# Edge phase of a graph-attention kernel: one f32 product for each query step and each relation step, with f32 one-hots

## What is computed

```python
mod_k  = K[src] + 0.2 * rel_w[edge_type][:, None, :]
scores = einsum('ehd,ehd->eh', Q[dst], mod_k) / 8
ex     = exp(scores - segment_max(scores, dst)[dst])
w      = ex / segment_sum(ex, dst)[dst]
agg    = segment_sum(w[:, :, None] * V[src], dst)
```

## Time and profile before

| | |
|---|---|
| median of three runs | 1356.09 us (1348.56 to 1357.88) |
| the profiled execution | 1346.19 us, span 1344.4 us |
| TensorE busy, share of the span | 1080.3 us, 80% |
| VectorE | 894.0 us, 66% |
| ScalarE | 666.2 us, 50% |
| GpSimd | 716.4 us, 53% |
| TensorE clock granted, mean | 0.868 of full speed |
| moved by DMA | 215.77 MB, mean 160 GB/s |

### The profile page before, as it was taken

How to read it: one execution, slowest core, us unless ns; L and a number is a source line. 1 busy time by engine, 2 the same in 40 slices (tenths; PEclk the granted TensorE clock), 3 DMA queues, 4 the chain that set the end, 5 groups by cost and what they waited for, 6 DMA issues and landing times.

```text
span 1344.4 us, 23897 instructions
## 1 busy us (share of the span) xinstructions
PE 1080.3 (80%) x7032; PEld 851.6 (63%) x7033; DVE 894.0 (66%) x1856; ACT 666.2 (50%) x2365; POOL 716.4 (53%) x714
## 2 busy tenths in 40 slices
PE   8978567776767777676677777799599999999997
PEld 3445345555545555555555565567389999999996
DVE  4767767677777877777777768889944444444443
ACT  5532356667667776576676766557511111111111
POOL 4455555555555655555556554756055555445663
PEclk9997777778888978777878878897699999999999
DMA  6266666656766666567666665602744444655332
GB/s 211 94 180 189 195 196 192 202 183 178 221 189 206 193 194 204 179 202 210 198 199 198 174 208 142 202 5 92 256 119 118 100 100 95 184 150 130 53 52 28
DMA packets 112993, 215.77 MB, mean 160 GB/s; under 512 B 19403, under 2 KB 57211, under 8 KB 112891
## 3 DMA queue, kind: packets, MB, share of 16 engines
q0 software_dynamic: 47488, 132.68, 36.7%
q1 hardware_dynamic: 59973, 80.16, 18.4%
q10 hardware_dynamic: 5430, 1.73, 0.6%
HBM read 191.96 MB, written 22.54 MB: 160 GB/s over the span
## 4 chain that ended last, share of the span: by engine, by line
PE 49%; DVE 21%; issue 16%; another core or an unknown queue 9%; ACT 2%; DMA 1%; DVEq 1%; SPq 0%; POOL 0%; POOLq 0%
PE qe_ps L1920 13%; PE bank L1929 8%; PE qe_ps L1732 6%; DVE ring L881 6%; PE bank L1772 5%; PE bank L1920 4%; DVE acc L893 3%; PE qe_ps L1772 2%; DVE ring L875 2%; DVE score L887 2%; PE qe_ps L1837 1%; PE qe_ps L1650 1%; PE qe_ps L1909 1%; PE bank L1650 1%
## 5 line engine op out<-in xcount | busy, mean ns | idle before, releaser
L632 POOL DMA_INDIRECT ring<-kv_table,src_idx x440 | 421.0, 957 | 330.4 <-DVE ring L881 181.5
L1502 ACT ACTIVATE wv<-ring,wgt 128x64 f32<-128x64 f32 x1628 | 407.3, 338 | 52.9 <-remote 46.5
L1732 PE MATMUL qe_ps<-q,hot_t 128*128 x1320 | 237.1, 316 | 140.0 <-issue 87.6
L1732 PEld LDWEIGHTS qe_ps<-q,hot_t 128*128 128x128 bf16 x1320 | 134.6, 110 | 209.0 <-issue 179.3
L1772 PE MATMUL bank<-wv,hotf 128*128 128x260 f32 x588 | 188.6, 451 | 25.2 <-issue 18.8
L697 POOL DMA_INDIRECT out<-room,slot_i x64 | 119.2, 1863 | 154.9 <-DMA out<-room,slot_i 81.4
L1920 PEld LDWEIGHTS qe_ps<-xg_t,ring 128*128 128x128 f32 x1536 | 181.4, 192 | 4.9 <-issue 1.7
L1621 ACT ACTIVATE act<-qe_ps 128x512 f32<-128x512 f32 x64 | 38.2, 597 | 294.7 <-PE bank L1920 140.9
L875 DVE TENSOR_TENSOR ring<-ring,bank 128x1024 f32<-128x1024 f32 x110 | 133.3, 1212 | 75.8 <-remote 63.3
L1920 PE MATMUL qe_ps<-xg_t,ring 128*128 128x128 f32 x1536 | 182.0, 275 | 1.3 <-issue 0.7
L881 DVE TENSOR_TENSOR ring<-ring,qe_ps 128x512 f32<-128x512 f32 x220 | 148.8, 677 | 26.1 <-remote 18.2
(11 more groups left out here) (339 smaller groups left out, 1504.5 us busy)
## 6 DMA issues: line engine op xcount, KB each, us to landing
ring<-in_w SPq DMA_DIRECT2D x48, 512.0 KB, 7.1
t_row<-t_rows SPq DMA_DIRECT2D x55, 256.0 KB
d_row<-d_rows SPq DMA_DIRECT2D x55, 256.0 KB
ring<-kv_table,src_idx POOLq DMA_INDIRECT x440
kv_table<-ring SPq DMA_DIRECT2D x25, 256.0 KB, 2.0
out<-acc SPq DMA_DIRECT2D x26, 128.0 KB, 1.7
x_table<-ring SPq DMA_DIRECT2D x26, 128.0 KB, 1.9
ring<-in_x SPq DMA_DIRECT2D x12, 256.0 KB, 9.0
```

Of the source, the lines that this page charges most:

```text
L632: pool.indirect_dma_start(ring[:, u, place(g) * D:(place(g) + 2) * D], None, kv_table, bass.IndirectOffsetOnAxis(ap=src_idx[:, 4 * g + u:4 ...
L1502: ins = act.activation(wv[:, g % WV_N, u, h, 0:HD], v_rows(g)[:, u, h * HD:(h + 1) * HD], ACT.Copy, scale=w[:, col:col + 1])
L1732: ins = pe.matmul(q_ps[p % AHEAD][:, u * D:(u + 1) * D], hot_t[:, p // 4 % HB_N, hot_cols(p, u)], tile_of(q3, q_tiles[p % 4])[:, k * D:(k ...
```

## The change

Queries are kept whole: `q_all`, f32, one copy from PSUM per tile by ScalarE (`keep_q`); the middle and low pieces, and VectorE's part in them, are gone. `hot_t` and `hot_r` become f32. `queries` makes one f32 product per step (two per pair), `relations` one f32 product per step with `rel_k`, `[64, 64]`; types, their one-hot and relation weights are on 64 partitions only. `turn_hot` still transposes bf16, reading the upper half of each f32 element. `hot_t` goes from seven buffers to six, and the copy of its first column for `factors` moves one octet ahead. Buffers move accordingly (`w_o`, `gamma`, `beta` and the gate's weights into `later`), and GpSimd no longer makes the relation's pieces. The core of the diff:

```diff
-HB_N = 7
+HB_N = 6
...
-        q3 = sb("q3", [P, NODE_TILES, 3 * D], BF16)
+        q_all = sb("q_all", [P, NODE_TILES, D])
+        later = sb("later", [P, KC * D + 2 * D + KC * NX + NX])
...
-        t_row = eb("t_row", [P, 8 * P], BF16)
-        hot_t = eb("hot_t", [P, HB_N, 8 * P], BF16)
-        hot_r = eb("hot_r", [P, 8 * P], BF16)
+        t_row = eb("t_row", [R, 8 * P], BF16)
+        hot_t = eb("hot_t", [P, HB_N, 8 * P])
+        hot_r = eb("hot_r", [R, 8 * P])
...
-                    c(pool.tensor_tensor(rel_r[:, :], rel02[:, :], rel_h[:, :], ALU.subtract))
-                    c(pool.tensor_copy(rel_m[:, :], rel_r[:, :]))
-                    c(pool.memset(rel_b[:, :], 0.0))
-                    c(pool.tensor_copy(rel_a[0:R, :], rel_h[0:R, :]))
-                    c(pool.tensor_copy(rel_a[R:P, :], rel_m[R:P, :]))
-                    c(pool.tensor_tensor(rel_b[0:R, :], rel_r[0:R, :], rel_m[0:R, :], ALU.subtract))
...
-                v.tensor_scalar(hot_r[:, :], t_row[:, :], part_r[:, 0:1], None, ALU.is_equal).then_inc(a_typ.sem, 1)
+                v.tensor_scalar(hot_r[:, :], t_row[:, :], part_r[0:R, 0:1], None, ALU.is_equal).then_inc(a_typ.sem, 1)
...
-            pieces_of_q(0, Q_FIRST)
...
                 if rows_due:
                     factor_rows(rows_due)
-                    v.tensor_copy(first[:, :], hot_t[:, rows_due * CS // 8 % HB_N, 0:1])
+                if maxima_due:
+                    v.tensor_copy(first[:, :], hot_t[:, maxima_due * CS // 8 % HB_N, 0:1])
...
-                sp.dma_start(t_row[:, :], bcast(t_rows[8 * m:8 * m + 8, :].rearrange("s c -> (s c)"))).then_inc(s_tr, 16)
+                sp.dma_start(t_row[:, :], bcast(t_rows[8 * m:8 * m + 8, :].rearrange("s c -> (s c)"), R)).then_inc(s_tr, 16)
...
-            def high_piece(t):
+            def keep_q(t):
                 s_q.wait(act, t)
-                act.activation(q3[:, t, 0:D], q_bank(t), ACT.Copy).then_inc(s_high.sem, 1)
...
+                act.activation(q_all[:, t, :], q_bank(t), ACT.Copy).then_inc(s_qk.sem, 1)
...
-                s_lo.wait(pe, min(p, NODE_TILES - 1))
+                s_qk.wait(pe, min(p, NODE_TILES - 1))
                 for u in range(2):
-                    for k in range(3):
-                        ins = pe.matmul(q_ps[p % AHEAD][:, u * D:(u + 1) * D], hot_t[:, p // 4 % HB_N, hot_cols(p, u)], tile_of(q3, q_tiles[p % 4])[:, k * D:(k + 1) * D],
-                                        start=(k == 0), stop=(k == 2))
+                    ins = pe.matmul(q_ps[p % AHEAD][:, u * D:(u + 1) * D], hot_t[:, p // 4 % HB_N, hot_cols(p, u)], tile_of(q_all, q_tiles[p % 4]), start=True, stop=True)
...
                 for u in range(8):
-                    for a in (rel_a, rel_b):
-                        ins = pe.matmul(rel_ps[:, u * HD:(u + 1) * HD], hot_r[:, u * P:(u + 1) * P], a[:, :], start=(a is rel_a), stop=(a is rel_b))
+                    ins = pe.matmul(rel_ps[:, u * HD:(u + 1) * HD], hot_r[:, u * P:(u + 1) * P], rel_k[:, :], start=True, stop=True)
...
-                    ins = pe.transpose(turn_ps.bitcast(BF16)[:, u * P:(u + 1) * P], hot_t[:, o % HB_N, u * P:(u + 1) * P], identb[:, :])
+                    ins = pe.transpose(turn_ps.bitcast(BF16)[:, u * P:(u + 1) * P], hot_t[:, o % HB_N, u * P:(u + 1) * P].bitcast(BF16)[:, 1::2], identb[:, :])
```

More of the change, by code:

```diff
@@ L294, in build @@
         rel = carve(acc_flat, HD)
-        rel02 = carve(acc_flat, HD)
-        rel_r = carve(acc_flat, HD)
         link_f = carve(acc_flat, CHUNKS * CS + 1)
         hop_f = carve(acc_flat, 2 * CHUNKS * CS).rearrange("p (i s) -> p i s", i=2)
-        rel_h = carve(acc_flat, HD // 2, BF16)
-        rel_m = carve(acc_flat, HD // 2, BF16)
         assert at[0] <= NT * H * HB
-        q3_flat = q3[:, :, :].rearrange("p t c -> p (t c)").bitcast(F32)
+        x_again = q_all[:, :, :].rearrange("p t c -> p (t c)")
+        xre = q_all[:, :, :]
         at[0] = 0
[L306 to L313, removed]
+        w_o = carve(later, KC * D).rearrange("p (k n) -> p k n", k=KC)
+        gamma = carve(later, D)
+        beta = carve(later, D)
+        gate_w = carve(later, KC * NX).rearrange("p (k n) -> p k n", k=KC)
+        gate_b = carve(later, NX)
         w_expert = flat[:, 0:WB * WX].rearrange("p (b n) -> p b n", b=WB)
@@ L357, in build @@
         typ = carve(hot_flat, STEPS // 2, BF16)
-        assert at[0] <= HB_N * 4 * P
+        first_row = carve(hot_flat, P)
+        last_row = carve(hot_flat, P)
+        iota_w = carve(hot_flat, P, I32)
+        iota_s = carve(hot_flat, 8, I32)
+        qe = carve(hot_flat, KC)
+        assert at[0] <= HB_N * 8 * P
         dst_t = late[0:PP, 0:4 * P].rearrange("p (q c) -> p q c", q=4)
@@ L457, in build @@
         s_xn, s_xt, s_enh, s_mm, s_ev, s_kv = (Count(sem(n)) for n in ("s_xn", "s_xt", "s_enh", "s_mm", "s_ev", "s_kv"))
-        s_q, s_high, s_rest, s_mid, s_lo = (Count(sem(n)) for n in ("s_q", "s_high", "s_rest", "s_mid", "s_lo"))
+        s_q, s_qk = (Count(sem(n)) for n in ("s_q", "s_qk"))
         s_kst = [sem(f"s_kst{i}") for i in range(NS)]
@@ L741, in _ @@
                 row_scales(i)
[L743 to L756, removed]
             v.wait_ge(s_qe, 32)
@@ L1281, in _ @@
                 sp.dma_start(tab_i[:, i, :, :], A[name].rearrange("(q p c) -> p q c", p=EP, c=P)).then_inc(landed, 16)
-            for i in range(2):
-                sp.dma_start(rel[i * R:(i + 1) * R, :], A["rel_w"]).then_inc(s_rel, 16)
+            sp.dma_start(rel[0:R, :], A["rel_w"]).then_inc(s_rel, 16)
             def load_nodes(m):
@@ L1422, in take @@
                 act.activation(kvq[:, t % NS, :], bank[3 + 2 * (t % 2)][:, :], ACT.Copy).then_inc(s_ev.sem, 1)
-            def high_piece(t):
+            def keep_q(t):
                 s_q.wait(act, t)
-                act.activation(q3[:, t, 0:D], q_bank(t), ACT.Copy).then_inc(s_high.sem, 1)
-            def middle_piece(t):
-                s_rest.wait(act, t)
-                act.activation(q3[:, t, D:2 * D], rest[:, t % 3, :], ACT.Copy).then_inc(s_mid.sem, 1)
+                act.activation(q_all[:, t, :], q_bank(t), ACT.Copy).then_inc(s_qk.sem, 1)
             row_roots(0)
@@ L1470, in steps_links @@
                 ins.then_inc(event("diffs").sem, 1)
-            for i in range(NODE_TILES + 1):
-                if i < NODE_TILES:
-                    high_piece(i)
-                if i >= 1 and i != Q_FIRST:
-                    middle_piece(i - 1)
+            for i in range(NODE_TILES):
+                keep_q(i)
                 if i == Q_FIRST - 1:
-                    middle_piece(i)
                     steps_links()
@@ L1659, in project_q @@
             def project_q(t):
-                s_rest.wait(pe, t - 3)
+                s_qk.wait(pe, t - 3)
                 for k in range(KC):
@@ L1776, in turn_scores @@
                 if ch == 0:
-                    s_rest.wait(pe, NODE_TILES - 1)
+                    s_qk.wait(pe, NODE_TILES - 1)
                 bank_free(("score", ch))
```

40 lines of the change are left out of this document (12 added, 28 removed).

## The result

The changed kernel takes 1495.36 us (median of 4, 1490.91 to 1497.03), the kernel before 1353.9 in the same job: ratio 1.104 [1.099, 1.109], or 141 us more. The forecast of 1388 (1300 to 1450) had the sign and missed the size. The profiled execution of the changed kernel took 1495.93 us, its span is 1494.2.

The account below looks back on a forecast made before the run. The edge stage was taken as bound by a loop of VectorE and TensorE with stalls, not one engine. +3.6 us per chunk in 12.6 chunks made +45, less 8 and 5: +32 us, so 1388 us, range 1300 to 1450.

Parts of the forecast that it names:

- Queries: TensorE, edge stage: six bf16 products become two f32 ones, 0.87 us per pair for 0.66, +0.85 us per octet.
- Relations: TensorE, edge stage: sixteen bf16 records become sixteen f32, 0.47 us to 1.75, +1.3 us per octet (bounds +0.4 and +1.6).
- Transposes: TensorE: eight bf16 transposes of the one-hot, now with a stride of two elements, take 0.45 us as before, +0.
- Compares: VectorE: a one-hot compare from bf16 to f32 takes 0.69 us, not 0.48; two per octet, +0.42 us.
- Pieces removed: VectorE, ahead of the loop and in its first four octets: 21 us of operations go, saving 8 us (bounds 0 and 21).
- The DMA term: Edge stage: 0.13 MB less of an octet's 2.7 MB to move, 0.1 us per octet, 5 us saved (0 to 20).
- The wait of the six buffers: VectorE's compare waits for TensorE's transposes of the same octet: 1.1 us, or 1.3 with the slower query; least 0.
- Its cover: Edge stage: stalls cover the added wait in half of the octets, dropping 2 x 1.3 us per chunk of four octets.
- (3): Edge stage: queries, relations, wait and compares all count in full, 3.9 us in 50 octets, about 1540 us; chance 0.05.
- (1): Edge stage: most TensorE stalls vanish as its loop slows, -34 to -71 us, about 1300 us; chance 0.20.
- (2): Edge stage: VectorE's 12 us of idle time per chunk absorb what is added, 1343 to 1364 us, say 1354; chance 0.20.
- The rule of the Trainium skill on instruction fetch: TensorE's code streams by its own DMA queue, mostly hidden, so an eighth fewer instructions is worth nothing; sum 19 us more.

Follow-up runs that it names:

- e11: The changed kernel, unchanged, in the faster kind of job: 1446.87 us beside 1165.81 for the kernel before, ratio 1.241.
- e15: The kernel before with six bf16 one-hot buffers in place of seven, nothing in f32, in the slower kind of job: 1.052 of the kernel before.
- e8: The changed kernel with its transposes in the octet's first slot in place of the third, six buffers, slower kind of job: 1.019 of the kernel before.
- e18: The changed kernel with transposes in the first slot and six buffers, run again in the slower kind of job: 1.031 of the kernel before.
- e7: The kernel before with only the relations changed to one f32 product, types on 64 partitions, slower kind of job: 1.002 of the kernel before.
- e16: The changed kernel with only queries in f32, relations in bf16, seven buffers, transposes in the first slot, slower kind of job: 1.024 of the kernel before.
- e2: The changed kernel with seven f32 one-hot buffers in place of six, all f32 work kept, faster kind of job: 1.030 of the kernel before.
- e3: The changed kernel with the compare for the node one-hots moved to the octet's end, six buffers, faster kind of job: 1.102 of the kernel before.

## Why the prediction was wrong in size

- **Queries** (+0.85 us per octet): four records per pair, 0.86 us (527.34 to 528.20 in the timeline), 0.87 forecast. Right.
- **Relations** (1.75 us, bounds to 2.1): 2.00 at full clock. Mis-sized by 0.25, inside the bounds.
- **Transposes** (0): 0.61 us for eight in either trace. The stride of two costs nothing. Right.
- **Compares** (0.69 us each): 0.77 and 0.74. Short by 0.13 per octet.
- **Pieces removed** (-8 us): the fifth octet's first `add_relation` starts at 148.59 us, before at 158.77. The first one starts 2.8 us earlier too, so the loop's first four octets gave 7.3. Right. That is with the f32 work of these octets in it. The DMA term (-5) can't be seen apart.
- **The wait of the six buffers: the step that failed.** Four parts of it.
  - *Its size without stalls*: the loop was put at 5.7 us of TensorE and 5.9 of VectorE, 11.6; e11's good octets take 12.9. TensorE's way is 6.7 us (from the end of the addition at 509.28 to 516.01): 0.6 is a pair's sums that stand in front of the relations, 0.25 the relations, 0.16 the tail of the transposes.
  - *Its cover*: "The stall of the rows begins right behind the transposes, so it covers the wait; I take that for half of the octets". It covers about a fifth. The wait alone, 65 us for 50 octets by the prediction's own 1.3, measured 70 (e15); I booked half. A reading that fits, and isn't shown: before, three banks of queries lay between the engines and took up part of a late result; the new wait asks for the newest result in every octet.
  - *The clock, put at nothing*: the terms of the sum are those of full clock, though the earlier trace rows had 0.82, and none is for more time at the lower level. Ten octets of the changed kernel (18.5 to 19.9 us, TensorE's way 10 to 11 us in place of 6.1) take about 33 us more than at 15.9 each.
  - *Its company*: wait and f32 work were added up. In the record's condition 70 us (e15) and 25 to 41 (e8 and e18, which stand in for the f32 work alone) make 95 to 111, and the change costs 141; where it is quiet, 90 and 37 make 127, and it costs 281. The 33 us of the long octets are about what is missing in the first sum; that they are the same thing isn't shown.
- **The rivals.** (3), "all adds up", came nearest and had 0.05 of the chance: it named 3.9 us per octet, and 3.1 were lost (16.8 less 13.7). It needed "stalls as long as now and behind none of the waits", and e15's idle times nearly add up in that way; but 1540 is too high, and it has no term for the clock either. (1), that stalls give way, was right in what it saw (TensorE's idle time with "issue" as the reason ahead of its query products was 83.2 us in 690 before and is 0 now) and wrong in what it would bring, since VectorE's wait ahead of L833 took its place. (2) holds for the relations alone (e7).
- **The rule of the Trainium skill on instruction fetch.** By it (page "Runtime: NRT & Kernel Launch", section "Instruction fetch mechanics") the sum was 19 us more, 1407, still far too low. Its consequence that fewer instructions are worth nothing agrees with e16, as far as that run tells. TensorE isn't starved by full DMA engines as such (e2 at 0.79). What delays its results in one condition and not in the other stays open. Nor is it shown that the lower clock is what turns 1.11 into 1.24.

## What to carry to other kernels

When a change takes a buffer from a ring, ask which instruction's result the producer then waits for, and whether it is issued in the same round; if it is, two engines that ran three deep run in lockstep, and each delay of one, a late result or a lower clock, is paid by both. Price that wait in every round, don't let a stall cover it, and look at several rounds before you say what a wait consists of: here some octets showed lateness and others a lower clock. Where the buffer can't be kept, move the awaited work to the front of its round: that one number, `TURN_SLOT`, was worth some 7 to 9% here, in the stalling condition, while all of the f32 products with it cost 2 to 3%.

## What the runs showed of the hardware

- The same program took 1164 us in one job and 1347 in another. In the slower kind of job the compare that waits for the transposes often starts well after their record ends (over 1 us in 17 of 41 octets of the changed kernel, up to 3.0, and in 33 of 45 in e15, up to 4.8); in the faster kind it starts 0.1 us after, in 40 of 43 (e11). The ratio of a change isn't the same in both: 1.10 and 1.24.
- With two engines waiting for each other in each octet, TensorE's granted clock was 0.65 in two octets of four (e11), and the same kernel with the compare moved had 0.95 over the stage (e3).
- Sixteen f32 products of 64 columns with 64 rows of weights take 2.00 us at full clock and 3.67 at the lower level.
- A compare of 1024 bf16 elements takes 0.77 us into f32 and 0.48 into bf16.
